# Attention's value product in a vision tower: nine streamed columns per head instead of 72

## The reference

```python
scores = jnp.einsum('bld,blwd->blw', q, k_w) / scale
attn = jax.nn.softmax(scores, axis=-1)
out = jnp.einsum('blw,blwd->bld', attn, v_w)
...
return out @ w_proj + b_proj
```

## Time and profile before

| | kernel before |
|---|---|
| median of 3 runs | 1084.4 us (1083.52 to 1084.65) |
| the profiled execution: its time | 1083.5 us |
| its span, from first to last instruction | 1081.6 us |
| TensorE busy (matmuls) | 979.3 us, 91% |
| TensorE weight loads | 623.9 us, 58% |
| VectorE busy | 617.2 us, 57% |
| ScalarE busy | 397.9 us, 37% |
| GpSimd busy | 151.4 us, 14% |
| mean granted clock of TensorE, share of full speed | 0.973 |

### The profile page before, as it was taken

How to read it: one execution, slowest core, us unless ns; L and a number is a source line. 1 busy time by engine, 2 the same in 40 slices (tenths; PEclk the granted TensorE clock), 3 DMA queues, 4 the chain that set the end, 5 groups by cost and what they waited for, 6 DMA issues and landing times.

```text
span 1081.6 us, 36566 instructions
## 1 busy us (share of the span) xinstructions
PE 979.3 (91%) x17004; PEld 623.9 (58%) x17004; DVE 617.2 (57%) x773; ACT 397.9 (37%) x522; POOL 151.4 (14%) x158
## 2 busy tenths in 40 slices
PE   4899899999989999999899899999899898688885
PEld 3667667657656533676567567656216687533342
DVE  2268457737833221587278357633143677769887
ACT  2432233224223486232332233224675567411100
POOL 6000000000000000000000000020010765334421
PEclk9999999999999899999999999999999899779998
DMA  5220230032022201310220220030001000000000
GB/s 196 93 78 3 69 90 17 3 105 67 4 90 102 59 6 40 109 30 3 93 78 4 78 87 9 4 100 10 14 14 44 2 2 1 2 1 1 2 11 10
DMA packets 25918, 46.78 MB, mean 43 GB/s; under 512 B 9949, under 2 KB 11000, under 8 KB 25125
## 3 DMA queue, kind: packets, MB, share of 16 engines
q1 hardware_dynamic: 24118, 42.47, 12.5%
q0 software_dynamic: 1456, 1.63, 0.6%
q10 hardware_dynamic: 192, 0.33, 0.1%
HBM read 30.25 MB, written 10.89 MB: 38 GB/s over the span
## 4 chain that ended last, share of the span: by engine, by line
PE 74%; DVE 12%; issue 5%; ACT 3%; POOL 3%; DMA 2%; SPq 1%; POOLq 0%; DVEq 0%
PE PSALL L1296 22%; PE PSALL L1264 7%; PE PSALL L1158 5%; PE PSALL L1287 5%; PE PSALL L1373 5%; PE PSALL L1239 4%; PE PSALL L1172 4%; PE PSALL L526 3%; PE PSALL L1383 3%; DVE WORK L1503 3%; PE PSALL L427 2%; DVE WORK L1003 2%; PE PSALL L513 2%; DVE WORK L1522 2%; PE PSALL L1135 2%
## 5 line engine op out<-in xcount | busy, mean ns | idle before, releaser
L1522 DVE STREAM_TRANSPOSE WORK<-PSALL 128x1024 f32<-128x1024 f32 x128 | 152.5, 1230 | 252.9 <-PE PSALL L1264 252.9
L1296 PEld LDWEIGHTS PSALL<-EW,WORK 128*64 128x64 f32 x4096 | 221.8, 138 | 72.8 <-issue 48.3
L1296 PE MATMUL PSALL<-EW,WORK 128*64 128x128 f32 x4096 | 247.6, 276 | 14.0 <-DVE WORK L1522 13.7
L1422 ACT ACTIVATE X<-PSALL,TABLES 128x1024 f32<-128x1024 f32 x128 | 141.8, 1114 | 307.2 <-PE PSALL L1296 307.2
L1503 DVE STREAM_TRANSPOSE WORK<-PSALL 128x1024 f32<-128x1024 f32 x84 | 104.3, 1242 | 32.8 <-PE PSALL L1158 30.9
L324 POOL DMA_DIRECT2D WORK<-MIXED x32 | 17.6, 550 | 670.5 <-ACT MIXED L1413 557.2
L1404 ACT COPY SPEC<-PSALL 128x400 f32<-128x400 f32 x64 | 54.4, 850 | 136.6 <-PE PSALL L1172 132.9
L1172 PEld LDWEIGHTS PSALL<-TABLES,WORK 128*64 128x64 f32 x2000 | 67.1, 138 | 48.8 <-DVE WORK L1503 31.4
L1003 DVE TENSOR_TENSOR WORK<-PSALL,X 128x832 f32<-128x832 f32 x80 | 79.3, 1017 | 16.8 <-PE PSALL L513 15.3
L1172 PE MATMUL PSALL<-TABLES,WORK 128*64 128x64 f32 x2000 | 80.7, 228 | 7.9 <-DVE WORK L1503 3.8
L1456 ACT ACTIVATE WORK<-PSALL,B 128x1024 f32<-128x1024 f32 x64 | 67.8, 1110 | 19.7 <-PE PSALL L1373 19.4
(11 more groups left out here) (157 smaller groups left out, 1157.7 us busy)
## 6 DMA issues: line engine op xcount, KB each, us to landing
SW<-in_spec_w SPq DMA_DIRECT2D x160, 80.0 KB, 2.8
spec_scr<-MIXED SPq DMA_DIRECT2D x24, 400.0 KB, 3.3
SPEC<-spec_scr SPq DMA_DIRECT2D x32, 200.0 KB
WORK<-spec_scr SPq DMA_DIRECT2D x16, 200.0 KB
WORK<-in_coords_w SPq DMA_DIRECT2D x2, 1024.0 KB, 4.8
XC<-in_coords_c SPq DMA_DIRECT2D x2, 1024.0 KB, 7.2
WORK<-MIXED SPq DMA_DIRECT2D x40, 40.0 KB
WORK<-MIXED POOLq DMA_DIRECT2D x32, 40.0 KB
```

The lines of the kernel that those rows point to most:

```text
L1296: m = pe.matmul(PS[2 * p + z][64 * j:64 * j + 64, 2 * b * GRID:(2 * b + 2) * GRID], G[:, n % 2, b, h:h + 2, :, t].rearrange("p q o -> p (q ...
L1422: nc.scalar.activation(X[:, n].rearrange("p b (z d) c w -> p d z b (c w)", z=2)[:, p, :, :, 2 * t * GRID:2 * (t + 1) * GRID], PSALL[:, 2 * ...
L1522: nc.vector.transpose(G[:, n % 2, 2 * x + y].rearrange("p h o v -> p o h v"), PSALL[:, 4 + 2 * x:6 + 2 * x, :].rearrange("p k (h o v) -> p ...
```

## The change

`values` streams and writes only the nine columns of the head itself:

```diff
                     at, v = (b % BC * HEADS + h) * VH, (b * HEADS + h) * VH
-                    m = pe.matmul(PS[6][0:TOK, at:at + HEADS * VH], PTZ[:, b % 2, h, :], VZ[:, v:v + HEADS * VH],
+                    m = pe.matmul(PS[6][0:TOK, at:at + VH], PTZ[:, b % 2, h, :], VZ[:, v:v + VH],
                                   start=True, stop=True)
                 m.then_inc(o_full, 1)
```

## The result

The changed kernel takes 1130.57 us (1130.16 to 1132.01, four runs) against 1084.53 us for the kernel before on the same chip: a ratio of 1.0449, 95% interval 1.0424 to 1.0475. It is 46 us slower, although it streams an eighth of the columns in 256 products and changes nothing else.

What follows compares the result with a forecast made beforehand. TensorE was taken to bound the attention loop. At the low clock its values, transposes, scores and smaller groups sum to 132.0 us instead of 81.7, +50.3 on the 1084.4 median: 1134 us, range 1104 to 1141.

Steps and rivals of the forecast that it cites:

- What bounds the loop: Attention loop, 846.2 to 928 us: TensorE bounds it, busy for 77.45 of 81.8 us.
- the cover that was claimed for VectorE, ScalarE and GpSimd: In the changed loop these engines need at most 59 of 132 us, so their work hides behind TensorE.
- Which clock: Clock falls at 842.7 us as before, does not rise at 849.6, and stays low until the expert stage.
- The comparison of two changed steps with the stretch from 839.3 to 846.2: Same scores and transposes, 8.0 against 6.9 us; the clock fell in that stretch, so it should stay low in the loop.
- The sum: First to last group of values at the low clock: 132.0 us instead of 81.7, so +50.3.
- The 110: Nanoseconds per nine-column values matmul at the low clock, giving groups of 1.90 us.
- The cost of a product: Values products: the 65-column weight load sets the pace, 59 ns a matmul at the high clock, 110 at the low.
- rival 3: Low clock in the loop, but loads at 59 ns: 1108 us; chance 0.08.
- Rival 1: Clock rises at 849.6 us as before and stays high through the loop: 1082.4 us, or 1070 with 34 ns; chance 0.10.
- Rival 2: Clock goes up and down, half of the loop at either level: about 25 us, 1109; chance 0.10.

Runs made afterwards that it cites:

- run 1: Changed kernel, but products of the first 8 images stream 72 columns, those of the other 24 nine: 1119.7 us.
- run 10: Changed kernel (nine columns) plus matmuls that nothing reads ahead of and behind the loop (steps 0 to 4 and 36 to 51): 1125.96 us.
- run 9: Kernel before, 72 columns, but products take only the 65 rows that hold probabilities, not the 63 zero rows: 1137.63 us.
- run 4: Kernel before with 63 columns in each product instead of 72: 1081.44 us, ratio 0.9998.
- run 6: Changed kernel, but 72 columns for four images, then nine with two unread 224-column matmuls a step: three executions 1101.95 to 1104.36 us, the fourth 1119.25.
- run 7: Kernel before, 72 columns, plus matmuls that nothing reads ahead of and behind the loop: 1077.70 us, ratio 0.9960.
- run 2: Changed kernel, but only the first 16 images stream nine columns, the last 16 stream 72: 1104.0 us.
- run 3: Changed kernel plus unread matmuls, 512 columns ahead of scores in steps 0 to 4, 224 ahead of each values group: 1116.2, 1153.2, 1154.9, 1158.0 us.

## Why the prediction was right, point by point

- **What bounds the loop.** TensorE, as read. Afterwards it has no gap in the loop, and the cover that was claimed for VectorE, ScalarE and GpSimd holds. The waits between 846 and 976 us, in us in total, times and longest, lead back to TensorE:

```profile
POOL SW L744 <- DVE smx L939: 68.1, 27, 3.9
ACT SW L645 <- PE PSALL L416: 44.5, 27, 3.2
DVE SW L935 <- PE PSALL L406: 40.3, 19, 3.4
```

- **Which clock.** The step with the most at stake, and right: low from 843 us, no rise in the loop, high again in the expert stage (0.66 on the mean from 1000 to 1010 us). The comparison of two changed steps with the stretch from 839.3 to 846.2 gave the right answer. That stretch had pauses, though, and so couldn't tell thin work from idle time; runs 1 and 10 do. And the comparison counted columns alone. Run 9 keeps all columns and loses the clock, so the rows that a product fills belong to the account.
- **The sum.** 132.0 us from the first group of values to the end of the last were forecast; it is 974.12 + 1.67 - 845.56 = 130.2. The groups of values measured 847.36 - 845.56 = 1.80 us instead of 1.90 (108 ns a matmul instead of 110, and nothing beyond), 32 x 0.10 = 3.2 less; transposes 0.94 instead of 0.91, 30 x 0.03 = 0.9 more; turns of four rows 0.48 instead of 0.44 (a group and a turn take 2.28 us, from 878.17 to 880.45), 10 x 0.04 = 0.4 more; scores 1.17 as said. The 110 was picked between 104 and 117 without a reason given, so that it came within 2 ns is luck in part; with 117 the forecast would have been some 4 us higher. The start is 0.7 us earlier, and what follows 928 us kept its length: 25.2 us from the last values to the first expert matmul, 24.5 before.
- **The cost of a product.** At the high clock 59 ns, taken from loads of equal width, is what run 4 shows with 63 columns; with nine, the groups of runs 1 and 6 come out at 57 and 58. At the low clock 108 decides against rival 3 (59): the load slows with the clock, its record from 137 ns to 232. The Trainium skill ("TensorE: Matmul & The Clock Gate", LDWEIGHTS) gives a load as its columns divided by 1.2, in ns, an estimate of 54 for these 65 columns, and names no clock with it; the trace is near that at the high clock (59) and at twice the figure at the low one (108).
- **Rival 1** (the clock stays) and the rule behind it are refuted by run 1. The Trainium skill ("TensorE: Matmul & The Clock Gate", HAM oscillation) puts the throttling down to idle gaps between bursts; here it came with TensorE busy for 7.00 of 7 us, then 1.78 of 2, then 11.00 of 11. The clock fell behind idle time too (at 931.5 us in the kernel before, and not where the profiled execution of run 7 had matmuls there), but idle time isn't the only cause.
- **Rival 2** (up and down) is not what the changed kernel does; the profiled execution of run 6 shows one such fall. That the median of run 6, 1104, is near the 1109 named for this rival is chance: it holds 56 added matmuls, and a loop that by its mean clock seems to have stayed high.
- **Why the low clock lasts.** That a slow loop puts less through the array per microsecond and so holds itself down is an argument that no run tests by itself, though runs 1, 2 and 10 fit it. What exactly the chip counts was not settled.

## What to carry to other kernels

Before a wide operand on TensorE is trimmed, ask what the surplus columns and rows do for the clock: in this dense loop the padding paid for 2.4 GHz, and all other matmuls of the loop paid when it went. Read the granted clock by stretch next to the busy share, since a slower TensorE looks busier. And cost a narrow matmul by its weight load: with loads of 65 columns next to nothing was left to gain below 63 columns, 59 ns with 63 and 57 to 58 with nine.

## What the runs showed of the hardware that was not expected

- Rows of zeros count. With 72 columns the loop ran at 2.4 GHz when the products filled 128 rows (63 of them zero), and at 1.2 GHz with 65 rows (run 9, executed once); the difference was 57 us in a kernel of 1081.
- The turn is quick both ways: the clock rose with the first wide group in a full loop (between 907.52 and 909.82 us in run 2) and fell behind the first thin one (between 867.35 and 870.31 in run 1).
- With a few wide matmuls beside the thin ones, one and the same program took 1116 to 1158 us (run 3, mean granted clock 0.950 to 0.912) or 1102 to 1119 (run 6, 0.975 to 0.956). What decides in one execution wasn't tried.
